# A four-layer gated decoder: first keys ahead of the ranks, returned rows signalled by choice, rounding and last tile on other engines

## The reference

```python
x = x + tanh(g_xattn[0]) * L0_xattn(ln(x), ctx)   # BiDAF: similarity, softmax, [x, s, x*s, x*mean] @ W
x = x + tanh(g_ffn[0])   * L0_ffn(ln(x))          # shared expert + top 2 of 8 experts:
    total = silu(flat @ w1_s) @ w2_s + sum_e cw[:, e:e+1] * (silu(flat @ w1[e]) @ w2[e])
x = x + tanh(g_xattn[1]) * L1_xattn(ln(x), ctx)   # 16 heads of 64: softmax(q k' / 8) v, @ Wo
x = x + tanh(g_ffn[1])   * L1_ffn(ln(x))          # int8-like: per-tensor scale, round, gelu, again
    scale = max(abs(x)) / 127; xq = round(x / scale); h = gelu((xq @ wq.T + b) * sw * sx); likewise w2
x = x + tanh(g_xattn[2]) * L2_xattn(ln(x), ctx, mask)  # 16 heads of 8, masked softmax, @ Wo + bo
x = x + tanh(g_ffn[2])   * L2_ffn(ln(x))          # ternary weights, int8-like rows: silu(gate) * up, down
x = x + tanh(g_xattn[3]) * L3_xattn(ln(x), ctx)   # one head
x = x + tanh(g_ffn[3])   * L3_ffn(ln(x))          # one expert of 8 for each batch: relu
```

## Time and profile before

| | |
|---|---|
| timed runs, median (lowest to highest) | 306.43 us (305.58 to 308.19), 3 runs |
| the profiled execution, its own time | 304.07 us |
| its span in the profile | 302.3 us |
| TensorE busy | 271.6 us, 90% |
| VectorE busy | 204.9 us, 68% |
| ScalarE busy | 151.0 us, 50% |
| GpSimd busy | 121.9 us, 40% |
| mean granted TensorE clock | 0.983 |

### The profile page before, as it was taken

The page is one execution under the profiler, slowest core; times in us unless marked ns, Lnnn a source line. Parts: engine busy times, 40 slices in busy tenths (PEclk is TensorE's granted clock), DMA queues, the critical chain, the costliest instruction groups (busy, mean ns, idle before and its releaser), DMA issues.

```text
span 302.3 us, 5461 instructions
## 1 busy us (share of the span) xinstructions
PE 271.6 (90%) x1930; PEld 197.1 (65%) x1930; DVE 204.9 (68%) x582; ACT 151.0 (50%) x333; POOL 121.9 (40%) x135
## 2 busy tenths in 40 slices
PE   8999887999989998779999979987999778879996
PEld 2578776799989974348888733544667543556475
DVE  2857899022821118999976458889999689988741
ACT  1220785522332366855454578148566745762331
POOL 6364227777756513345354100206653602421100
PEclk9999998999999999799999998999999999999999
DMA  6970407998897132095000100000000000000002
GB/s 173 356 252 1 141 22 249 345 295 236 240 313 256 35 94 64 4 358 194 2 1 2 69 0 2 0 0 0 2 4 0 2 0 0 2 0 3 0 8 64
DMA packets 17912, 28.65 MB, mean 95 GB/s; under 512 B 3632, under 2 KB 10494, under 8 KB 17886
## 3 DMA queue, kind: packets, MB, share of 16 engines
q1 hardware_dynamic: 15972, 25.12, 24.7%
q0 software_dynamic: 1536, 3.02, 3.9%
q10 hardware_dynamic: 378, 0.16, 0.3%
HBM read 25.21 MB, written 3.08 MB: 94 GB/s over the span
## 4 chain that ended last, share of the span: by engine, by line
PE 51%; DVE 24%; ACT 8%; DMA 6%; issue 6%; POOL 2%; SPq 1%; POOLq 0%; DVEq 0%; ACTq 0%
PE bank L1263 6%; PE bank L1326 6%; PE bank L1255 6%; PE bank L1003 4%; DVE pmax L1901 4%; DVE pr L1902 4%; PE bank L1030 4%; DVE psums L1908 3%; PE bank L1309 3%; PE bank L1223 3%; DMA w_router<-in_w_router 2%; DMA yt<-acc,back 2%; ACT pr L840 2%; DMA pr<-lnd,source 2%; PE bank L1548 1%
## 5 line engine op out<-in xcount | busy, mean ns | idle before, releaser
L577 POOL TENSOR_TENSOR rstd<-var,minus_half 128x4 f32<-128x4 f32 x16 | 16.5, 1030 | 70.7 <-DVE var L1597 70.5
L602 POOL TENSOR_TENSOR pr<-pr,psums 128x1232 f32<-128x1232 f32 x12 | 27.0, 2248 | 34.4 <-DVE psums L1910 34.4
L1030 PE MATMUL bank<-onesb,identb 128*128 128x512 bf16 x121 | 32.8, 395 | 0.0
L694 ACT ACTIVATE prT<-bank 128x512 f32<-128x512 f32 (+1 forms) x48 | 22.0, 486 | 20.9 <-PE bank L1003 20.6
L799 ACT ACTIVATE prT<-bank 128x512 f32<-128x512 f32 x23 | 13.7, 598 | 31.6 <-PE bank L1255 31.6
L1901 DVE TENSOR_REDUCE pmax<-bank 128x6 f32<-128x462 f32 (+1 forms) x48 | 26.9, 560 | 3.0 <-PE bank L1313 1.8
L1866 DVE COPY acc<-bank 128x128 f32<-128x128 f32 x23 | 6.7, 291 | 32.0 <-PE bank L1263 24.9
L656 POOL DMA_INDIRECT yt<-acc,back x23 | 22.8, 990 | 11.6 <-DVE acc L1866 7.0
L1003 PE MATMUL bank<-ident,pr 128*128 128x128 f32 (+1 forms) x140 | 21.8, 286 | 5.0 <-ACT prT L697 3.4
L1255 PE MATMUL bank<-prT,experts 128*128 128x128 f32 x184 | 25.1, 281 | 0.5 <-issue 0.5
L1263 PE MATMUL bank<-experts,prT 128*128 128x128 f32 x184 | 24.2, 276 | 0.9 <-DVE acc L1866 0.9
(11 more groups left out here) (356 smaller groups left out, 578.3 us busy)
## 6 DMA issues: line engine op xcount, KB each, us to landing
experts<-in_w SPq DMA_DIRECT2D x23, 512.0 KB, 5.2
experts<-in_w SPq DMA_DIRECT2D x2, 2048.0 KB
lnd<-ln SPq DMA_DIRECT2D x4, 256.0 KB, 2.6
experts<-yt SPq DMA_DIRECT2D x4, 256.0 KB, 3.0
x<-in_x SPq DMA_DIRECT2D x2, 256.0 KB, 3.9
wkv<-in_wk SPq DMA_DIRECT2D x1, 512.0 KB, 6.9
wkv<-in_wv SPq DMA_DIRECT2D x1, 512.0 KB, 6.4
wqT<-in_wqT SPq DMA_DIRECT2D x1, 512.0 KB, 7.0
```

The lines of the kernel that those rows point to most:

```text
L602: pool.tensor_tensor(v, v, psums[:, n % 4, 1, :].unsqueeze(2).to_broadcast([P, H, R]), ALU.mult).then_inc(p_ready, 1)
L694: ins = act.activation(dst[:, c0:full, :], bank[:, 0:(full - c0) * P].rearrange("p (c k) -> p c k", k=P), ACT.Copy)
L1030: pe.matmul(bank[:, :].rearrange("p (c k) -> p c k", c=C), identb[:, :], onesb[:, :].unsqueeze(1).to_broadcast([P, C, P]), start=True, sto ...
```

## The change

- Layer 1's keys are made ahead of the ranks, where 5 idle matmuls stood, and `kv2` and `k3` ahead of `perm`. `SH_EARLY` is 2: two of the shared expert's four groups stand ahead of the expert loop, and its second half begins with block 2.
- SP signals the returned rows of batch 0 for each choice. It fetches batch 1's once choice 0 has landed, and VectorE combines choice by choice. `values_1(1)` goes from ahead of the L1x transposes to between the scores of tiles 0 and 1, and on ScalarE behind batch 1's scaling.
- The 2 idle matmuls ahead of `total_max(0)` go, and 8 become 4 ahead of L1f's second layer.
- ScalarE rounds batch 1 in halves and also writes it to `hqb`, with a semaphore of its own.
- In the last tile of layer 2's attention, Exp and sums go bank by bank; VectorE multiplies in two halves in GpSimd's place, and the first two chunks of transposes wait for one half each. ScalarE's table load stands behind the last chunk's copy.

```diff
@@ -47,3 +47,3 @@
 PAIRS = 3
-SH_EARLY = 0
+SH_EARLY = 2
 F2 = 0
@@ -108,8 +108,8 @@
     t += [("xT", b) for b in range(B)]
-    s.append("rank")
     s += [("kv1", 0, i) for i in range(3)]
+    s.append("rank")
     t += [("lnT", "L0f", b) for b in range(B)]
     s += [("kv1", 1, i) for i in range(3)]
-    s.append("perm")
     s += ["kv2", "k3"]
+    s.append("perm")
     s += [("m1", i + h) for i in range(PAIRS) for h in (0, PAIRS)]
@@ -135,5 +135,7 @@
     o += [("shy", 1)]
-    t += [("n1", b, i) for b in range(B) for i in range(len(TCH))]
+    t += [("n1", 0, i) for i in range(len(TCH))]
     for layer in ("L1x", "L2x"):
         t.append(("lnT", layer, 0))
+        if layer == "L1x":
+            t += [("n1", 1, i) for i in range(len(TCH))]
         for n in range(T):
@@ -388,3 +390,3 @@
         y_stored = [sem(f"y{i}_stored") for i in range(4)]
-        y_back = [sem(f"y_back{b}") for b in range(B)]
+        y_back = [sem(f"y_back{k}_0") for k in range(K2)] + [sem("y_back_1")]
         pen_ready = sem("pen_ready")
@@ -411,2 +413,4 @@
         p_exp = sem("p_exp")
+        part_exp = sem("part_exp")
+        p_last = sem("p_last")
         p_recip = sem("p_recip")
@@ -417,2 +421,3 @@
         hq_ready = sem("hq_ready")
+        h1q_ready = sem("h1q_ready")
         q_scale = sem("q_scale")
@@ -518,8 +523,14 @@
                 sp.wait_ge(y_stored[i], 16 * len(range(i, NB, 4)))
-            for b in range(B):
-                for k in range(K2):
-                    r = k * T * P + b * SEQ
-                    sp.dma_start(gy[:, k, b * TB:b * TB + TB, :],
-                                 yt[r:r + SEQ, :].rearrange("(t p) d -> p t d", p=P)).then_inc(y_back[b], 16)
-                sp.wait_ge(y_back[b], 16 * K2)
+            def fetch_back(b, k, sem_):
+                r = k * T * P + b * SEQ
+                sp.dma_start(gy[:, k, b * TB:b * TB + TB, :],
+                             yt[r:r + SEQ, :].rearrange("(t p) d -> p t d", p=P)).then_inc(sem_, 16)
+
+            for k in range(K2):
+                fetch_back(0, k, y_back[k])
+            sp.wait_ge(y_back[0], 16)
+            for k in range(K2):
+                fetch_back(1, k, y_back[K2])
+            sp.wait_ge(y_back[1], 16)
+            sp.wait_ge(y_back[K2], 16 * K2)
 
@@ -671,3 +682,3 @@
             add_bias("L2x", bo2, 2)
-            normalise("L2x", 2, T)
+            normalise("L2x", 2, T - 1)
             inverse_root("L2f")
@@ -813,6 +824,5 @@
             load_table(2, ACT.Exp)
-            values_1(1)
             transposed("L1x", 0)
             act.wait_ge(pw_ready, 1)
-            act.wait_ge(y_back[1], 16 * K2)
+            act.wait_ge(y_back[K2], 16 * K2)
             for k in range(K2):
@@ -821,2 +831,3 @@
                                    scale=pw[:, k, t:t + 1]).then_inc(scaled, 1)
+            values_1(1)
 
@@ -841,2 +852,10 @@
 
+                def exps_by_bank(n):
+
+                    for i, (h0, h1) in enumerate(HEADS):
+                        v = pr4[n % 4][:, h0 * R:h1 * R]
+                        act.wait_ge(*S.freed((layer, n, i)))
+                        act.activation(v, v, ACT.Exp, scale=rstd[:, n:n + 1]).then_inc(
+                            part_exp if i < len(HEADS) - 1 else p_exp, 1)
+
                 def queries(b):
@@ -856,5 +875,6 @@
                         if i == len(TCH) - 1 and n + 2 < T:
-                            exps(n + 2)
                             if n + 3 == T and layer == "L2x":
-                                load_table(*after)
+                                exps_by_bank(n + 2)
+                            else:
+                                exps(n + 2)
                         copy_chunks(("pT", layer, n, i), prT[:, n % 2, :, :], c0, c1)
@@ -864,6 +884,5 @@
                         copy_out(O, ("L2x", 0), o2T[:, 0, :], O.bank(("L2x", 0))[:, :])
+                load_table(*after)
                 if layer == "L2x":
                     copy_out(O, ("L2x", 1), o2T[:, 1, :], O.bank(("L2x", 1))[:, :])
-                else:
-                    load_table(*after)
 
@@ -895,4 +914,8 @@
             act.wait_ge(h_scale, 1)
-            act.activation(hT[:, 1, :, :], hT[:, 1, :, :], ACT.Identity, bias=magic[:, :],
-                           scale=wsc[:, 10:11]).then_inc(h_rounded, 1)
+            for i in range(2):
+                act.activation(hT[:, 1, :, i * 2 * P:(i + 1) * 2 * P], hT[:, 1, :, i * 2 * P:(i + 1) * 2 * P],
+                               ACT.Identity, bias=magic[:, :], scale=wsc[:, 10:11]).then_inc(h_rounded, 1)
+                act.wait_ge(h_rounded, i + 1)
+                act.activation(hqb[:, :, SEQ + i * 2 * P:SEQ + (i + 1) * 2 * P], hT[:, 1, :, i * 2 * P:(i + 1) * 2 * P],
+                               ACT.Identity, bias=less_magic[:, :]).then_inc(h1q_ready, 1)
             attention("L2x", (5, ACT.Silu))
@@ -1175,4 +1198,5 @@
 
+            pe.wait_ge(*loaded("wk1"))
+            keys_values_1(0)
             bank = acquire(S, "rank")
-            idle_work(bank, 5)
             takenf = taken[:, :, :].rearrange("p t e -> p (t e)")
@@ -1186,4 +1210,2 @@
 
-            pe.wait_ge(*loaded("wk1"))
-            keys_values_1(0)
             pe.wait_ge(*loaded("l1x"))
@@ -1193,2 +1215,9 @@
 
+            pe.wait_ge(*loaded("l2x"))
+            bank = acquire(S, "kv2")
+            pe.matmul(bank[:, 0:B * R], w2x[:, 1, :], ctxTf, start=True, stop=True)
+            pe.matmul(bank[:, B * R:2 * B * R], w2x[:, 2, :], ctxTf, start=True, stop=True).then_inc(S.full("kv2"), 1)
+            pe.wait_ge(*loaded("l3x"))
+            bank = acquire(S, "k3")
+            pe.matmul(bank[:, 0:B * R], w3x[:, 1, :], ctxTf, start=True, stop=True).then_inc(S.full("k3"), 1)
             bank = acquire(S, "perm")
@@ -1204,9 +1233,2 @@
 
-            pe.wait_ge(*loaded("l2x"))
-            bank = acquire(S, "kv2")
-            pe.matmul(bank[:, 0:B * R], w2x[:, 1, :], ctxTf, start=True, stop=True)
-            pe.matmul(bank[:, B * R:2 * B * R], w2x[:, 2, :], ctxTf, start=True, stop=True).then_inc(S.full("kv2"), 1)
-            pe.wait_ge(*loaded("l3x"))
-            bank = acquire(S, "k3")
-            pe.matmul(bank[:, 0:B * R], w3x[:, 1, :], ctxTf, start=True, stop=True).then_inc(S.full("k3"), 1)
             per_head("m1", 0, wqT1, 0, PAIRS)
@@ -1368,4 +1391,8 @@
                         transpose_rows(layer, 1)
-                    pe.wait_ge(p_ready, T * (layer == "L2x") + n + 1)
+                    last = layer == "L2x" and n == T - 1
+                    if not last:
+                        pe.wait_ge(p_ready, T * (layer == "L2x") + n + 1)
                     for i, (c0, c1) in enumerate(TCH):
+                        if last and i < 2:
+                            pe.wait_ge(p_last, i + 1)
                         if layer == "L2x" and n == 1 and i == 1:
@@ -1403,3 +1430,2 @@
             values_2(1)
-            idle_work(acquire(S, ("maxT", 0)), 2)
             total_max(0)
@@ -1422,3 +1448,3 @@
             total_max(1)
-            idle_work(acquire(TR, ("lnT", "L2x", 0)), 8)
+            idle_work(acquire(TR, ("lnT", "L2x", 0)), 4)
             for b in range(B):
@@ -1428,3 +1454,3 @@
                     if t % 2 == 0:
-                        pe.wait_ge(hq_ready, n // 2 + 1)
+                        pe.wait_ge(h1q_ready if b else hq_ready, t // 2 + 1)
                     for c in range(C):
@@ -1841,4 +1867,4 @@
             def combine(b):
-                dve.wait_ge(y_back[b], 16 * K2)
                 for k in range(K2):
+                    dve.wait_ge(y_back[k], 16)
                     for t in range(b * TB, b * TB + TB):
@@ -1911,2 +1937,17 @@
 
+                def last_probabilities(n):
+
+                    rows = pr4[n % 4].rearrange("p (h r) -> p h r", h=H)
+                    for i, (h0, h1) in enumerate(HEADS):
+                        if i < len(HEADS) - 1:
+                            dve.wait_ge(part_exp, i + 1)
+                        else:
+                            dve.wait_ge(p_exp, base + n + 1)
+                        ins = dve.tensor_reduce(psums[:, n % 4, 0, h0:h1], rows[:, h0:h1, :], AX, ALU.add)
+                    step(ins)
+                    step(dve.reciprocal(psums[:, n % 4, 1, :], psums[:, n % 4, 0, :]))
+                    for h in range(0, H, H // 2):
+                        v = rows[:, h:h + H // 2, :]
+                        dve.tensor_tensor(v, v, bc(psums[:, n % 4, 1, h:h + H // 2], R), ALU.mult).then_inc(p_last, 1)
+
                 for i in range(len(HEADS)):
@@ -1918,3 +1959,6 @@
                             less_max(n + 1, i)
-                    sums(n)
+                    if layer == "L2x" and n == T - 1:
+                        last_probabilities(n)
+                    else:
+                        sums(n)
                     if n + 1 < T:
@@ -1969,7 +2013,2 @@
                 dve.tensor_scalar(hqb[:, :, i * 2 * P:(i + 1) * 2 * P], v, MAGIC, None, ALU.subtract).then_inc(hq_ready, 1)
```

(5 more changed lines are left out.)

4 lines of the change are left out of this document (2 added, 2 removed).

## The result

The changed kernel takes 302.03 us (median of 4 executions, 301.6 to 303.4), the kernel before on the same chip 306.0 (4 executions, 305.06 to 308.19): ratio 0.9882, 95% interval 0.9833 to 0.993. A second set on another occasion gave 302.53 against 306.35, 0.9886 (0.9834 to 0.9937). So the medians make the change worth about 1.2%, 3.8 to 4.0 us; the interval runs from 2.1 to 5.1 us, and the 2.85 of the forecast lie in it. Faster by over 1% had a chance of 0.42, within 1% of 0.51.

A forecast was written before the change was run, and what follows sets the result against it. No engine was full end to end; around 84 to 90 us GpSimd and its DMAs held the loop. Terms 0 - 1.2 - 0.9 - 0.3 + 0.5 - 0.95 = -2.85 took the median 306.43 to 303.6, range 301.3 to 306.9.

The forecast's parts named there:

- Loop: Expert loop: two shared groups ahead of it and full clock shorten the wait for scatter 8; -1.2 us, range 0 to -3.
- Rival 1: Ahead of the loop: early keys and shared groups don't help, scatter 8 lands at 90.2 as before; 304.8 us, chance 0.22.
- Routing: Routing stage: first keys ahead of the ranks leave GpSimd's first gather at 42.91; 0 us, bound +0.5.
- Returned rows: Behind the loop: combining by choice and moving values_1(1) start the L1x transposes 1.2 us sooner, 0.3 handed back; net -0.9.
- Two idle matmuls: Ahead of total_max(0): dropping two idle matmuls gains 0.3 us, range 0 to -0.5.
- ScalarE's rounding: Second L1f layer: four ScalarE instructions for batch 1 make its last matmuls end later; +0.5 us, range -0.1 to +1.0.
- Last tile: Last attention tile: batch 1's update starts sooner, VectorE then late; -0.95 us, between 0.4 and 1.4 gained.
- Rival 2: Expert loop: the landing shortens and TensorE's lead counts in full, -3 in place of -1.2; 301.8 us, chance 0.15.
- Rival 3: After 187: TensorE stays at the low clock level for one stretch more, costing 1.9 us; 305.4 us, chance 0.13.
- Rival 4: After 187: TensorE's low clock level holds until the second attention runs, costing some 5 us; 308.6 us, chance 0.08.

The follow-up runs named there:

- keys_back: Changed kernel with the part ahead of the loop undone (ranks first, 5 idle matmuls, kv2 and k3 behind perm, SH_EARLY 0); 301.82 us, ratio 0.9884.
- part_returned: Kernel before with only the returned rows signalled by choice and values_1(1) behind the scores of tile 0; 320.31 us, ratio 0.997.
- ahead10: Changed kernel with AHEAD 10 in place of 14, so fewer gathers ahead of GpSimd's first scatter; 320.94 us, ratio 1.003.
- rounding_back8: Changed kernel with the whole rounding edit undone: one ScalarE instruction, VectorE subtracts, 8 idle matmuls; 302.49 us, ratio 0.9878.
- after_again: Changed kernel, unedited, measured again beside the kernel before; 302.53 us against 306.35, ratio 0.9886.
- part_last: Kernel before with only the last attention tile changed: Exp by bank, sums and halved multiply on VectorE, table load behind last copy; 319.61 us, ratio 0.9964.

## Why the prediction was right, and where it wasn't

The median is 302.03, inside the range and 1.6 below the forecast; the sign and every term but the loop's hold. The sum came near with luck, by two errors of opposite sign: one in a term, and one in how the sum was carried over to the median. The second is as sure as the medians are, within about 1 us.

- **Loop, -1.2: the step that failed.** The full clock after 50 and TensorE's lead came as forecast (3.0 us at `block_down` 11, where 3.5 was the bound), and scatter 8 landed at 89.2, near 89 as I wrote. But I asked only when scatter 8 lands, and not which scatters hold TensorE once it is ahead. Scatter 6 takes 2.53 us of the lead and scatter 7 the rest. Their landings aren't shorter: scatter 6's takes 6.85 us (before 5.3 at most), scatter 7's 6.68 (before 5.88, from 80.49 to VectorE's copy at 86.39; 6.6 in keys_back). And one block more is behind the hold. Measured: some 0.6 in place of 1.2, and none that the timed executions tell. Rival 1 had nearly the size (0 for this part), with another reason: scatter 8 itself did move.
- **Routing, 0: right.** The ranks start at 34.70, not 34.49, with 0.31 us of idle time in front of them; of that the execution is 0.11 later by itself ahead of the routing, and 0.1 is the edit's.
- **Returned rows, -1.2 and +0.3 back.** -0.9 to -1.2 (A), and nothing handed back: tile 1's first maximum comes 0.2 later behind the scores (0.4 was worked out), but the Exp of tile 0, which is next on the path, doesn't wait for it. The combine's 0.8 is right.
- **Two idle matmuls, -0.3.** -0.37 (B). They had no run of their own, but in the runs of the other parts B doesn't move at full clock (18.15, 18.16), so they are what is left.
- **ScalarE's rounding, +0.5.** +0.66 at full clock, and +0.53 against the profiled execution before, whose C had a piece of low clock. From the scale to the last L1f matmul it is 5.41 us, as forecast (5.4). The four instructions took 1.24, 1.15, 1.23 and 1.15, where I took 1.15 each.
- **Last tile, -0.95.** -1.10 (D). VectorE is late next, as forecast. The output copy starts 13.5 us behind the tile's first maximum (14.6 before, 13.2 by the forecast), but that isn't what ends it.
- **Rivals 2, 3 and 4** didn't happen in this kernel: the landings that hold TensorE aren't shorter, and TensorE is at the 2.4 GHz level from 185 to 195. With VectorE's form of the rounding and 4 idle matmuls a thing like rival 3 was seen (C 11.40). Rival 3's terms give 305.5, not 305.4.
- **From the profiled execution to the median.** The terms that the stages show add up to some -1.8 to -2.4 (A -1.1, B -0.37, C +0.6, D -1.1, the loop 0 to -0.6, 0.2 lost in the second attention, which part_returned and ahead10 show too and keys_back and rounding_back8 don't, and whose cause wasn't found); the profiled pair differs by 2.2, the medians by 3.8 to 4.0. I set the forecast 2.85 below the median as if both kernels' profiled executions stood alike to their medians. They didn't: before's was 2.4 below its median, the changed kernel's 0.2. In the last set the mean clock of the 11 executions of before is 0.981 and their mean span 304.2, of after_again's six 0.990 and 300.9: a difference of 3.25 in the mean, with an uncertainty of about 1. Part of it goes with fewer stretches at the low level; but a dip isn't always paid for: keys_back has one at 50, where GpSimd and the scatters set the pace, and is as quick as after_again. At a like clock the gap is near the sum of the stages. At 0.982 and 0.983 the spans of before are 303.4 to 305.9, mean 304.9, and those of the last set's four kernels 302.1 and 302.8. At 0.988 and 0.989 they are 301.5 and 302.1 against eleven of 299.6 to 301.8, mean 300.6. That is 2.4 and 1.2 us; the rest of the 3.8 goes with a higher mean clock. What in the change raises the clock, if anything does, isn't shown, and how much is stages and how much clock stays open within about 1 us.

## What to carry to other kernels

When an edit gives an engine a lead over a ring of buffers, don't ask how much sooner the slot that blocks it today comes free: count which slots it now asks for sooner, when those land and how much work is left behind them. Time a small edit by the length of its own stage between two landmarks, which repeated to 0.03 us here in three stages of four, and not by the whole, which moves by several us with the clock. A forecast against one profiled execution needs that execution's place in the spread of its own kernel before it is carried over to a median. Where two engines can share the last step of a chain, give each a half by its measured time, not all of it to the one that looks idle.

## What the runs showed of the hardware

On two other chips every kernel took 13 to 14 us more, nearly all ahead of the fetch (121.5 to 125.3, not 107.5 to 109.1). In these traces several engines stand at once where the loop begins, for 2 to 9 us each, and the trace names no releaser. ScalarE, TensorE and GpSimd in part_last ("remote" is another core or an unknown queue):

```profile
51.83 0.56 ACT L690 ACTIVATE pr<-bank 128x462 f32<-128x462 f32 x1 [4.34 <-remote]
...
53.91 1.40 PE L1084 MATMUL bank<-hT,wo 64*128 64x154 f32 x8 [5.26 <-issue]
...
60.40 1.64 ACT L690 ACTIVATE pr<-bank 128x462 f32<-128x462 f32 x4 [6.59 <-remote]
...
60.84 0.95 POOL L646 DMA_INDIRECT pr<-lnd,source  x1 [2.36 <-remote]
```

TensorE is busy 6.15 of 17 us in 43 to 60 there, 14.82 in the first pair's kernel before. The copies ScalarE stands in front of need only a filled bank, which TensorE had filled long before. At the start of the loop it happens in every one of the eight profiles of these chips and in none of the six others, with and without the early keys. What they wait for wasn't found.

ScalarE takes 1.24 or 1.23 us for 1024 columns with a scale, in place, 1.15 for the same to bf16, and 2.10 for 2048 columns in one instruction: two halves cost 0.3 more than the whole. VectorE's subtraction of the same 1024 columns takes 0.69. What a stretch of low clock costs depends on where it lies. The row 250 to 260 of part_returned has 0.83, in stage D, which took 1.14 us more (17.71, not 16.57). From the first score of the first attention to batch 0's update, before, keys_back and ahead10 have a row of 0.83 and take 43.64 or 43.65 us, as rounding_back8 does at full clock; after_again has one too and takes 44.17. At 50, where GpSimd and the scatters set the pace, such a stretch cost nothing that the runs show.
